# Edge passes of a graph network with one transposed scan per slot, a ring of four row slots and direct indices

## The chip, the cores and the metric

The kernel runs on one core of one Trainium2 chip. The metric is the device time of one execution in microseconds (us). The kernel before takes 10,483.51 us (median of three runs, 10,478.12 to 10,493.6). TensorE, VectorE, ScalarE and GpSimd compute; the Sync, ScalarE and GpSimd queues issue DMAs. Engines are ordered against each other by counting semaphores alone.

## What is computed

Four blocks of a graph network are applied to the same 6,250 nodes of 96 numbers, over 200,000 edges sorted by their destination. Each block's result is added to its input and normalised.

```python
x = _layernorm(x + gat(x, ...))      # attention over edges: softmax by destination, 4 heads of 24
x = _layernorm(x + egnn(x, ...))     # twice: maximum by destination of x[src] @ W_msg + edge_attr @ W_edge
x = _layernorm(x + sage(x, ...))     # twice: mean by destination of x[src]
x = _layernorm(x + gcn(x, ...))      # three times: weighted sum by destination
```

In the attention block an edge's logit is `e = leaky_relu(a_src[src] + a_dst[dst], 0.2)`, and `exp(e - max)` weighs the row `h[src]`, with sum and maximum over the edges of one destination. In the second block `agg = segment_max(x[src] @ W_msg + edge_attr @ W_edge, dst)`.

## The kernel before

The edges are padded to 128 x 1,568: each of the 128 partitions holds 1,568 edges in order of destination. So a running value (maximum, or a weighted sum rescaled when the maximum rises) can go along a partition from edge to edge, and a large negative number in `reset` stops it where a new destination starts. The value behind each edge is stored to DRAM (`hist0`, `hist`), and the row of each node's last edge is gathered from there behind the pass (line 477, 49 indirect DMAs); `carries` then joins what runs over from one partition to the next.

There are three such **gather passes**: the attention pass (q = 0) and two maximum passes (q = 1, 2). A pass works in 196 **slots** of S = 8 edges a partition. For each slot GpSimd issues eight indirect DMAs (line 455), each fetching one row of the node table for each partition, into one of two halves of `G`. Their indices are a copy that ScalarE makes (`idx`, line 923) when it has done the slot's other work, and GpSimd waits for it (line 450) and for VectorE's `rows_used` (line 452).

In an attention slot VectorE adds up the logits (L1341, L1342), runs four scans of eight (L1344), prepares two exponents which ScalarE evaluates (L917), multiplies the eight rows (L1356), and then goes through the eight edges one by one: scale the previous state (L1362), add it (L1365), each step waiting for the one before. The result lies in a second pair of buffers, `H`, which the Sync queue stores (L547). In the first 25 slots VectorE also does a piece of other preparation (`table_piece`).

In a maximum slot there is more. TensorE multiplies eight tiles of edge attributes (L687), which VectorE adds to the gathered rows (L1395), and eight dependent steps `max(previous + reset, row)` follow (L1399). Beside this each slot does four steps (CS = 4) of **counting**: for the later passes the kernel builds a table of how many edges go from a node to a node, as sums of products of one-hot tiles. VectorE compares to make these tiles (L1388, wide, and L1389, narrow), ScalarE makes four scaled identities (L904), TensorE adds three products into PSUM (L666, L667, L672), the third of which takes the previous step's sum, so that ScalarE must have copied this sum (L911) first. Each sum is then flushed to a row of DRAM whose number the Sync queue loads from a table (L541, L542). All engines work in order. The Sync queue's order in a slot is four flushes, the store, the load of the edge attributes for the slot after next (L556).

ScalarE's and GpSimd's passes are loops of the chip; VectorE's and the Sync queue's are written out in full. The seven passes of the mean and graph-convolution blocks behind 8,642 us use the count table and gather nothing.

## Time and profile before

| | us |
|---|---|
| median of three runs | 10,483.51 |
| the profiled execution | 10,478.01 |
| its span | 10,475.3 |
| TensorE, VectorE, GpSimd, ScalarE busy | 4,947.4, 5,313.2, 4,906.2, 1,468.9 |
| DMA moved | 1,134 MB |

The profile divides the span by engine and line, says for each instruction how long its engine had been idle and which event ended this, and gives the order of events in any stretch. "Remote" is what it calls an event whose origin it does not know. A DMA's issue is the queue's work, and its landing a separate event. GpSimd's DMA instructions last about 0.95 us and start 1.25 us apart; the time from start to start is what counts. Three stretches matter: the attention pass from 207 to 2,572 us, and the maximum passes from 2,858 to 5,690 and from 5,812 to 8,642. Behind them TensorE is busy most of the time.

### The profile page before, as it was taken

What the parts mean: (1) busy time and instruction counts of PE and PEld (TensorE: products, weight loads), DVE (VectorE), ACT (ScalarE), POOL (GpSimd) and SP (SyncE); (2) the same over time, 40 slices, a digit from 0 to 9 for tenths busy, and PEclk for the clock granted to TensorE, in tenths of its full rate; (3) what the DMA queues carried; (4) which work ended last, traced back from release to release, by engine and by line L of the source; (5) the groups of instructions that cost most, each with busy time, mean ns of one, the idle gap of its engine ahead of it and who ended that gap; (6) DMA issues with size and microseconds to landing.
All of it is one profiled execution on the core that took longest, in us unless ns stands there. A gap on an engine that the chain in (4) does not pass through costs nothing.

```text
span 10475.3 us, 121795 instructions
## 1 busy us (share of the span) xinstructions
PE 4947.4 (47%) x25358; PEld 3490.2 (33%) x25358; DVE 5313.2 (51%) x17848; ACT 1468.9 (14%) x4065; POOL 4906.2 (47%) x5030
## 2 busy tenths in 40 slices
PE   1100000000355555555554555555555554999999
PEld 1000000000233332322322322322233234999999
DVE  4766665565644444444443544444444446632224
ACT  0000000000122222222221222222222220000000
POOL 6766666666155555555555455555555552000000
PEclk5555555555555555555555555555555557999999
DMA  4322222222033333333332333333333333676666
GB/s 130 87 71 71 72 71 70 72 71 66 27 94 92 92 91 92 92 93 91 92 93 72 89 92 91 94 91 94 92 92 92 92 100 106 217 266 226 227 227 242
DMA packets 605562, 1134.21 MB, mean 108 GB/s; under 512 B 165250, under 2 KB 372501, under 8 KB 604904
## 3 DMA queue, kind: packets, MB, share of 16 engines
q1 hardware_dynamic: 408198, 679.86, 19.3%
q0 software_dynamic: 159184, 251.10, 12.1%
q10 hardware_dynamic: 37906, 200.73, 4.8%
q14 instruction: 240, 1.97, 0.1%
q8 instruction: 34, 0.56, 0.0%
HBM read 716.84 MB, written 414.33 MB: 108 GB/s over the span
## 4 chain that ended last, share of the span: by engine, by line
PE 34%; another core or an unknown queue 27%; DVE 19%; issue 11%; ACT 3%; ACTq 3%; POOL 2%; DMA 1%; DVEq 0%; POOLq 0%; SPq 0%
PE psO L687 7%; PE psB L710 5%; PE psA L710 5%; DVE CG L1365 5%; DVE SCR L1362 5%; PE psX L710 5%; PE psB L672 3%; PE psA L672 2%; PE psA L666 2%; DVE CG L1356 2%; PE psA L667 2%; POOL CG L455 2%; ACT BUF L904 2%; DVE Rm L1344 1%
## 5 line engine op out<-in xcount | busy, mean ns | idle before, releaser
L455 POOL DMA_INDIRECT CG<-table,idx x4704 | 4567.6, 971 | 3678.5 <-issue 1737.8
L1395 DVE TENSOR_TENSOR CG<-CG,psO 128x384 f32<-128x384 f32 x784 | 433.9, 554 | 2475.0 <-remote 2401.0
L672 PE MATMUL psB<-BUF 128*128 128x392 bf16 x784 | 366.2, 467 | 2369.8 <-ACT BUF L911 2279.6
L687 PE MATMUL psO<-WE,BUF 32*128 32x96 f32 x6272 | 1328.8, 394 | 102.4 <-issue 91.9
L687 PEld LDWEIGHTS psO<-WE,BUF 32*128 32x128 f32 x6272 | 1242.9, 298 | 230.6 <-issue 230.6
L1388 DVE TENSOR_SCALAR BUF<-iota,EG 128x392 bf16<-128x392 f16 x3136 | 1050.0, 335 | 221.7 <-issue 160.0
L1399 DVE SCALAR_TENSOR_TENSOR CG<-CG,BUF 128x96 f32<-128x96 f32 x3136 | 1000.8, 319 | 159.0 <-DVE CG L1395 20.2
L672 PEld LDWEIGHTS psB<-BUF 128*128 128x128 bf16 x784 | 81.4, 104 | 2879.3 <-issue 2879.3
L753 PE MATMUL psA<-ident,F 128*100 128x128 f32 x1 | 0.5, 452 | 2091.7 <-DVEq L1320 2091.7
L911 ACT CAST BUF<-psA 128x392 bf16<-128x392 f32 x784 | 381.1, 486 | 3669.8 <-remote 2748.8
L1389 DVE TENSOR_SCALAR BUF<-iota,EG 128x128 bf16<-128x128 f16 x3136 | 771.1, 246 | 6.9 <-issue 6.7
L753 PEld LDWEIGHTS psA<-ident,F 128*100 128x100 f32 x1 | 0.2, 158 | 2092.1 <-DVEq L1320 2092.1
L440 POOL CAST CG<-EG x35 | 26.1, 744 | 1381.1 <-DVEq L1091 1381.1
L1365 DVE TENSOR_TENSOR CG<-CG,SCR 128x100 f32<-128x100 f32 x1568 | 415.4, 265 | 209.9 <-DVE SCR L1362 133.6
L1362 DVE TENSOR_TENSOR SCR<-CG,EX 128x100 f32<-128x100 f32 x1568 | 414.4, 264 | 208.3 <-DVE CG L1365 114.8
L904 ACT ACTIVATE BUF<-ident,EG 128x128 bf16<-128x128 f32 x1568 | 501.5, 391 | 68.0 <-issue 50.9
L710 PE MATMUL psB<-CG,BUF 128*128 128x288 bf16 x4018 | 508.5, 287 | 0.8 <-POOL CG L443 0.8
L710 PE MATMUL psA<-CG,BUF 128*128 128x288 bf16 x4018 | 508.3, 287 | 1.0 <-POOL CG L443 1.0
L710 PE MATMUL psX<-CG,BUF 128*128 128x288 bf16 x3969 | 500.8, 286 | 0.0
L710 PEld LDWEIGHTS psB<-CG,BUF 128*128 128x128 bf16 x4018 | 494.9, 142 | 2.9 <-POOL CG L443 1.1
L710 PEld LDWEIGHTS psA<-CG,BUF 128*128 128x128 bf16 x4018 | 494.8, 142 | 3.0 <-POOL CG L443 1.2
L710 PEld LDWEIGHTS psX<-CG,BUF 128*128 128x128 bf16 x3969 | 488.3, 142 | 1.0 <-POOL CG L443 0.3
(259 smaller groups left out, 5869.2 us busy)
## 6 DMA issues: line engine op xcount, KB each, us to landing
BUF<-counts SPq DMA_DIRECT2D x245, 784.0 KB, 5.8
BUF<-counts ACTq DMA_DIRECT2D x245, 784.0 KB, 6.4
counts<-BUF SPq DMA_DIRECT2D x1572, 98.0 KB
hist<-CG SPq DMA_DIRECT2D x394, 384.0 KB
hist<-CG SPq DMA_DIRECT2D x198, 416.0 KB
CG<-table,idx POOLq DMA_INDIRECT x4704
BUF<-in_edge_attr SPq DMA_DIRECT2D x392, 128.0 KB
table<-TB SPq DMA_DIRECT2D x14, 336.0 KB
```

The source lines that it names most:

```text
L455: pool.indirect_dma_start(out=G[:, s, k * width:(k + 1) * width], out_offset=None, in_=tab, in_offset=bass.IndirectOffsetOnAxis(ap=idx[:, ...
L672: pe.matmul(sums, KI[:, j, :], ACC[:, (j - 1) % CS, :], start=False, stop=True).then_inc(counted, 1)
L687: mm = pe.matmul(ETERM[:, s, k // 4, (k % 4) * DIM:(k % 4 + 1) * DIM], EA[:, s, k, :], WE[:, n0 // ITERS, :], start=True, stop=True)
L710: mm = pe.matmul(sums[:, 0:3 * DIM], CNT16[:, B % 3, b:b + NB * (P - 1) + 1:NB], PARTS[:, b, :], start=b == 0, stop=b == NB - 1, skip_grou ...
L904: nc.scalar.activation(KI[:, j, :], ident[:, :], ACT.Copy, scale=STEP[:, 4, bass.ds(i * (2 * CS) + (s * CS + j), 1)]).then_inc(keep_ready, 1)
L911: nc.scalar.copy(ACC[:, j, :], psM[j % 2][:, 0:CW]).then_inc(acc_ready, 1)
L1362: link(tt(scaled_state[:, :].rearrange("p (h w) -> p h w", w=HW), prev_state(H0, s, k, SW).rearrange("p (h w) -> p h w", w=HW), EX[:, 0, k ...
L1365: link(tt(H0[:, s, k, 0:SW], H0[:, s, k, 0:SW], scaled_state[:, :], ALU.add))
L1388: ts(RHS[:, j, a, :], iota16[:, :], STEP[:, a, column], None, ALU.is_equal).then_inc(onehot_ready, 1)
L1389: ts(LO[:, j, a, :], iota16[:, 0:P], STEP[:, 2 + a, column], None, ALU.is_equal).then_inc(onehot_ready, 1)
L1395: link(tt(HWD[:, s, ks, :], GW[:, s, ks, :], ETERM[:, s, h, 0:4 * DIM].rearrange("p (k w) -> p k w", w=DIM), ALU.add))
L1399: link(stt(HWD[:, s, k, :], prev_state(HWD, s, k, DIM), reset[:, u * S + k:u * S + k + 1], HWD[:, s, k, :], ALU.add, ALU.max))
```

## The change

- The eight dependent steps of a slot become **one scan** over all columns. The slot is laid out transposed, nine elements a column: the last value of the previous slot and the eight new ones. The boundary of a column is a factor of zero (attention) or a large negative reset (maximum), so that one scan instruction runs over 100 x 9 or 96 x 9 elements. VectorE writes its product or addition transposed into `state_cols` or `max_cols`; ScalarE copies the scanned values back into row order (`rows_back`), and spreads resets and factors over the columns (`column_resets`, `head_resets`, `scales`). The four scans of the heads become one, too, and the logits of a slot are computed one slot ahead.
- `G` and `H` become **one ring of four slots**, `ROWS0` or `ROWSW`: the rows are gathered into a slot, the results are written over them, and the slot is stored from there. GpSimd waits only for the landing of the store of four slots ago.
- The gathers take their **indices directly** from the array of sources; `idx` and ScalarE's copy of it go. GpSimd's and ScalarE's passes are written out in full.
- The narrow one-hot tiles of a slot are made by one comparison in place of eight.
- The last two of a slot's four **flushes** are issued by ScalarE behind its sums, in place of the Sync queue, and the row number's range is no longer asserted.

The core of the diff (the old bodies are in the listing above):

```diff
+HOTS = 1 + 2 * CS
+RING = 4
+LAPS = SLOTS // RING
+assert LAPS * RING == SLOTS
+K9 = S + 1
...
+    ROWS0 = CG[:, 0:RING * S * W0].rearrange("p (r k w) -> p r k w", r=RING, k=S)
+    ROWSW = CG[:, 0:RING * S * DIM].rearrange("p (r k w) -> p r k w", r=RING, k=S)
...
+    terms = sb("terms", [P, 2, HEADS, K9])
+    maxima = sb("maxima", [P, 1 + HEADS * K9])
+    max9 = maxima[:, 1:].rearrange("p (h k) -> p h k", k=K9)
+    EX = sb("EX", [P, 2, 2, HEADS, K9])
+    reset_heads = sb("reset_heads", [P, 2, HEADS, K9])
+    spread1 = sb("spread1", [P, DIM * K9])
...
+    state_cols = [STG[:, 0:SW * K9].rearrange("p (c k) -> p c k", k=K9), XTQ[:, 0:SW * K9].rearrange("p (c k) -> p c k", k=K9)]
+    max_cols = [STG[:, 0:DIM * K9].rearrange("p (c k) -> p c k", k=K9), XTQ[:, 0:DIM * K9].rearrange("p (c k) -> p c k", k=K9)]
+    max_flat = [STG[:, 0:DIM * K9], XTQ[:, 0:DIM * K9]]
+    scales_flat = XTQ[:, SW * K9:2 * SW * K9]
+    reset_flat = [XTQ[:, SW * K9:SW * K9 + DIM * K9], spread1[:, :]]
+    reset_cols = [v.rearrange("p (c k) -> p c k", k=K9) for v in reset_flat]
...
-        def gather_pass(q, tab, width):
-            with pool.Fori(0, ITERS) as i:
...
+        def gather_pass(q, tab, rows_in):
+            for u in range(SLOTS):
+                r, lap = u % RING, q * LAPS + u // RING
+                if u >= RING:
+                    pool.wait_ge(hist_stored[r], 16 * lap)
+                for k in range(S):
+                    pool.indirect_dma_start(
+                        out=rows_in[:, r, k, :], out_offset=None, in_=tab,
+                        in_offset=bass.IndirectOffsetOnAxis(ap=SRC[:, u * S + k:u * S + k + 1], axis=0)).then_inc(
+                            gathered[r], 16)
...
-                for j in range(CS):
+                for j in range(CS // 2):
                     k = u * CS + j
                     sp.wait_ge(acc_ready, m * HALF + k + 3)
-                    row = sp.value_load(ADDR[0:1, k:k + 1], min_val=0, max_val=TRASH + BG - 1)
+                    row = sp.value_load(ADDR[0:1, k:k + 1])
                     sp.dma_start(counts16[bass.ds(row, P, BG), :], ACC[:, j, :]).then_inc(flushed[j], 16)
             def store(u):
-                s = u % 2
-                sp.wait_ge(block_done[s], u // 2 + q * ITERS + 1)
-                sp.dma_start(rec[:, u * S * width:(u + 1) * S * width], H[:, s, 0:S * width]).then_inc(hist_stored[s], 16)
+                r, lap = u % RING, q * LAPS + u // RING
+                sp.wait_ge(block_done[r], lap + 1)
+                sp.dma_start(rec[:, u * S * width:(u + 1) * S * width], ring[:, r, :]).then_inc(hist_stored[r], 16)
...
-                    pe.wait_ge(rows_used[s], i + (q * ITERS + 1))
+                    pe.wait_ge(eterm_used, i * 2 + (m * SLOTS + s + 1))
...
+        def count_steps(m, u):
+            k0 = m * HALF + u * CS
+            act.wait_ge(counted, k0 + 1)
             for j in range(CS):
                 nc.scalar.activation(KI[:, j, :], ident[:, :], ACT.Copy,
-                                     scale=STEP[:, 4, bass.ds(i * (2 * CS) + (s * CS + j), 1)]).then_inc(keep_ready, 1)
+                                     scale=STEP[:, 4, u * CS + j:u * CS + j + 1]).then_inc(keep_ready, 1)
             for j in range(CS):
-                act.wait_ge(counted, i * (2 * CS) + (m * HALF + s * CS + j + 2))
-                act.sem_inc(turn["act"], 1)
-                act.wait_ge(flushed[j], i * 32 + 16 * (m * 2 * ITERS + s + 1))
-                act.sem_inc(turn["act"], 1)
+                act.wait_ge(flushed[j], 16 * (m * SLOTS + u + 1))
+                act.wait_ge(counted, k0 + j + 2)
                 nc.scalar.copy(ACC[:, j, :], psM[j % 2][:, 0:CW]).then_inc(acc_ready, 1)
-        def edge_pass(q):
...
+            for j in range(CS // 2, CS):
+                act.wait_ge(acc_ready, k0 + j + 3)
+                row = act.value_load(ADDR[0:1, u * CS + j:u * CS + j + 1])
+                act.dma_start(counts16[bass.ds(row, P, BG), :], ACC[:, j, :]).then_inc(flushed[j], 16)
+        def attention_pass():
+            def head_resets(u):
+                nc.scalar.copy(reset_heads[:, u % 2, :, 1:K9],
+                               reset[:, u * S:(u + 1) * S].unsqueeze(1).broadcast_to([P, HEADS, S])).then_inc(resets_ready, 1)
+            def rows_back(u):
+                nc.scalar.copy(ROWS0[:, u % RING, :, 0:SW],
+                               state_cols[u % 2][:, :, 1:K9].rearrange("p c k -> p k c")).then_inc(block_done[u % RING], 1)
+            act.wait_ge(out_ready, NG)
+            act.wait_ge(pass_begun, 1)
+            head_resets(0)
+            head_resets(1)
+            for u in range(SLOTS):
+                act.wait_ge(exp_in, u + 1)
+                nc.scalar.activation(EX[:, u % 2, :, :, :], EX[:, u % 2, :, :, :], ACT.Exp).then_inc(exp_done, 1)
+                if u + 2 < SLOTS:
+                    head_resets(u + 2)
+                if u:
+                    act.wait_ge(scanned, u)
+                act.wait_ge(exp_done, u + 1)
+                nc.scalar.copy(scales[:, :, 1:K9].rearrange("p (h w) k -> p h w k", w=HW),
+                               EX[:, u % 2, 0, :, 1:K9].unsqueeze(2).broadcast_to([P, HEADS, HW, S])).then_inc(scales_ready, 1)
+                if u:
+                    rows_back(u - 1)
...
+            act.wait_ge(scanned, SLOTS)
+            rows_back(SLOTS - 1)
...
+        def running_pass(f, q):
+            m = MAX_PASSES.index(q)
+            def column_resets(u):
+                nc.scalar.copy(reset_cols[u % 2][:, :, 1:K9],
+                               reset[:, u * S:(u + 1) * S].unsqueeze(1).broadcast_to([P, DIM, S])).then_inc(resets_ready, 1)
+            def rows_back(u):
+                nc.scalar.copy(ROWSW[:, u % RING, :, :],
+                               max_cols[u % 2][:, :, 1:K9].rearrange("p c k -> p k c")).then_inc(block_done[u % RING], 1)
+            act.wait_ge(out_ready, out_group_base(f, "rows") + NG)
+            act.wait_ge(pass_begun, q + 1)
+            act.wait_ge(steps_loaded, 32 * (m + 1))
+            column_resets(0)
+            column_resets(1)
+            for u in range(SLOTS):
+                if u:
+                    act.wait_ge(scanned, q * SLOTS + u)
+                    rows_back(u - 1)
+                    if u + 1 < SLOTS:
+                        column_resets(u + 1)
+                count_steps(m, u)
+            act.wait_ge(scanned, (q + 1) * SLOTS)
+            rows_back(SLOTS - 1)
...
+            def logits(u):
+                r, b = u % RING, u % 2
                 here = slice(u * S, (u + 1) * S)
...
+                z = terms[:, 1, :, 1:K9]
+                dve.wait_ge(gathered[r], 16 * S * (u // RING + 1))
+                link(tt(z.rearrange("p h k -> p k h"), ROWS0[:, r, :, SW:W0], AD[:, here, :], ALU.add))
+                step(stt(z, z, 0.2, z, ALU.mult, ALU.max))
+                dve.wait_ge(resets_ready, u + 1)
+                dve.wait_ge(dve_step, steps[0])
+                link(nc.vector.tensor_tensor_scan(
+                    out=maxima[:, 1:], data0=reset_heads[:, b, :, :].rearrange("p h k -> p (h k)"),
+                    data1=terms[:, 1, :, :].rearrange("p h k -> p (h k)"), initial=0.0, op0=ALU.add, op1=ALU.max))
+                link(tt(terms[:, 0, :, :].rearrange("p h k -> p (h k)"), maxima[:, 0:HEADS * K9],
+                        reset_heads[:, b, :, :].rearrange("p h k -> p (h k)"), ALU.add))
+                tt(EX[:, b, :, :, :].rearrange("p a h k -> p a (h k)"), terms[:, :, :, :].rearrange("p a h k -> p a (h k)"),
+                   maxima[:, 1:].unsqueeze(1).broadcast_to([P, 2, HEADS * K9]), ALU.subtract).then_inc(exp_in, 1)
+                step(nc.vector.tensor_copy(ROWS0[:, r, :, SW:W0], max9[:, :, 1:K9].rearrange("p h k -> p k h")))
+                dve.wait_ge(exp_in, u + 1)
+                step(nc.vector.tensor_copy(terms[:, 1, :, 0:1], max9[:, :, S:K9]))
+            def states(u):
+                r, b = u % RING, u % 2
+                if u >= 2:
+                    dve.wait_ge(block_done[(u - 2) % RING], (u - 2) // RING + 1)
+                dve.wait_ge(exp_done, u + 1)
+                step(tt(state_cols[b][:, :, 1:K9].rearrange("p (h w) k -> p h w k", w=HW),
+                        ROWS0[:, r, :, 0:SW].rearrange("p k (h w) -> p h w k", w=HW),
+                        EX[:, b, 1, :, 1:K9].unsqueeze(2).broadcast_to([P, HEADS, HW, S]), ALU.mult))
+                if u:
+                    dve.wait_ge(scanned, u)
+                step(nc.vector.tensor_copy(state_cols[b][:, :, 0:1], state_cols[1 - b][:, :, S:K9]))
+                dve.wait_ge(scales_ready, u + 1)
+                dve.wait_ge(dve_step, steps[0])
+                nc.vector.tensor_tensor_scan(out=state_flat[b], data0=scales_flat, data1=state_flat[b], initial=0.0,
+                                             op0=ALU.mult, op1=ALU.add).then_inc(scanned, 1)
+            link(nc.vector.memset(scales[:, :, 0:1], 0.0))
+            link(nc.vector.memset(state_cols[1][:, :, S:K9], 0.0))
+            dve.sem_inc(pass_begun, 1)
+            logits(0)
             for u in range(SLOTS):
-                slot(u)
+                if u + 1 < SLOTS:
+                    logits(u + 1)
+                states(u)
...
+                r, b = u % RING, u % 2
                 dve.wait_ge(counted, m * HALF + u * CS + 1)
+                tt(LO, iota16[:, 0:P].unsqueeze(1).unsqueeze(1).broadcast_to([P, CS, 2, P]),
+                   STEP[:, 2:4, u * CS:(u + 1) * CS].rearrange("p a j -> p j a").unsqueeze(3).broadcast_to([P, CS, 2, P]),
+                   ALU.is_equal).then_inc(onehot_ready, 1)
                 for j in range(CS):
-                    column = slice(u * CS + j, u * CS + j + 1)
                     for a in range(2):
-                        ts(RHS[:, j, a, :], iota16[:, :], STEP[:, a, column], None, ALU.is_equal).then_inc(onehot_ready, 1)
-                        ts(LO[:, j, a, :], iota16[:, 0:P], STEP[:, 2 + a, column], None, ALU.is_equal).then_inc(onehot_ready, 1)
-                dve.wait_ge(gathered[s], 16 * S * (q * ITERS + i + 1))
-                dve.wait_ge(hist_stored[s], 16 * (q * ITERS + i + 2))
+                        ts(RHS[:, j, a, :], iota16[:, :], STEP[:, a, u * CS + j:u * CS + j + 1], None,
+                           ALU.is_equal).then_inc(onehot_ready, 1)
+                if u:
+                    dve.wait_ge(scanned, q * SLOTS + u)
+                step(nc.vector.tensor_copy(max_cols[b][:, :, 0:1], max_cols[1 - b][:, :, S:K9]))
+                dve.wait_ge(gathered[r], 16 * S * (q * LAPS + u // RING + 1))
                 dve.wait_ge(eterm_ready[s], m * ITERS + i + 1)
-                for h in range(2):
-                    ks = slice(4 * h, 4 * h + 4)
-                    link(tt(HWD[:, s, ks, :], GW[:, s, ks, :],
-                            ETERM[:, s, h, 0:4 * DIM].rearrange("p (k w) -> p k w", w=DIM), ALU.add))
-                dve.sem_inc(rows_used[s], 1)
-                for k in range(S):
-                    link(stt(HWD[:, s, k, :], prev_state(HWD, s, k, DIM), reset[:, u * S + k:u * S + k + 1],
-                             HWD[:, s, k, :], ALU.add, ALU.max))
-                dve.sem_inc(block_done[s], 1)
+                if u >= 2:
+                    dve.wait_ge(block_done[(u - 2) % RING], q * LAPS + (u - 2) // RING + 1)
+                tt(max_cols[b][:, :, 1:K9].rearrange("p c (a k) -> p c a k", a=2),
+                   ROWSW[:, r, :, :].rearrange("p (a k) c -> p c a k", a=2),
+                   ETERM[:, s, :, 0:4 * DIM].rearrange("p a (k c) -> p c a k", c=DIM), ALU.add).then_inc(eterm_used, 1)
+                dve.wait_ge(resets_ready, q * SLOTS + u + 1)
+                dve.wait_ge(dve_step, steps[0])
+                dve.wait_ge(eterm_used, m * SLOTS + u + 3)
+                nc.vector.tensor_tensor_scan(out=max_flat[b], data0=reset_flat[b], data1=max_flat[b], initial=0.0,
+                                             op0=ALU.add, op1=ALU.max).then_inc(scanned, 1)
+            dve.wait_ge(scanned, (q + 1) * SLOTS)
+            dve.wait_ge(block_done[RING - 1], (q + 1) * LAPS)
```

## Rows read from the trace of the kernel before

**Rows 1.** Table of stages: stretch, its length, busy us of each engine (and count).

```profile
207.00:2572.00 2365.00, 47.31 (x204) 22.53 (x204) 1485.02 (x5603) 78.40 (x392) 1524.83 (x1568) 0.51 0.28 72
...
2858.00:5690.00 2832.00, 1557.38 (x5553) 858.25 (x5553) 1390.64 (x5105) 640.87 (x1764) 1533.35 (x1576) 0.53 0.33 92
```

**Rows 2.** Timeline of GpSimd in a maximum pass: start, length, instruction, [idle before <- releaser].

```profile
4000.46 1.09 POOL L455 DMA_INDIRECT CG<-table,idx  x1 [8.53 <-ACT idx L923]
4001.85 1.17 POOL L455 DMA_INDIRECT CG<-table,idx  x1 [0.30 <-issue]
...
4019.70 0.95 POOL L455 DMA_INDIRECT CG<-table,idx  x1 [0.30 <-issue]
4028.94 1.09 POOL L455 DMA_INDIRECT CG<-table,idx  x1 [8.29 <-ACT idx L923]
```

**Rows 3.** Table of stretches within that cycle, columns as in Rows 1.

```profile
4011.00:4023.30 12.30, 0.36 (x2) 0.00 (x0) 0.00 (x0) 0.00 (x0) 7.51 (x8) 0.50 0.35 95
```

**Rows 4.** Timeline of VectorE (DVE) and ScalarE (ACT) in that cycle.

```profile
4023.34 1.14 DVE L1395 TENSOR_TENSOR CG<-CG,psO 128x384 f32<-128x384 f32 x2 [12.46 <-remote]
4023.52 0.49 ACT L911 CAST BUF<-psA 128x392 bf16<-128x392 f32 x1 [14.01 <-remote]
...
4027.46 0.49 ACT L911 CAST BUF<-psB 128x392 bf16<-128x392 f32 x1 [0.83 <-PE psB L672]
...
4035.89 0.49 ACT L911 CAST BUF<-psB 128x392 bf16<-128x392 f32 x1 [0.67 <-issue]
```

**Rows 5.** Sync queue's flush steps, 4023 to 4030, then 4006 to 4023: ns min/median/max.

```profile
L541 SPq TENSOR_LOAD <-EG x4: 266/286/349, 4024.0 to 4028.0; - x4
L542 SPq DMA_DIRECT2D counts<-BUF x4: 332/338/355, 4024.7 to 4028.8; - x4
...
L542 SPq DMA_DIRECT2D counts<-BUF x3: 699/699/702, 4008.3 to 4021.0; - x3
```

**Rows 6.** Timeline behind the first maximum pass, while GpSimd gathers end rows.

```profile
5690.37 1.86 PE L770 MATMUL psO<-SCR,SEL 128*128 128x96 bf16 x21 [3.94 <-issue]
5718.64 0.86 DVE L1458 TENSOR_TENSOR CG<-psO,cpen 128x672 f32 x1 [28.62 <-remote]
```

**Rows 7.** Timeline of GpSimd in the attention pass.

```profile
1503.86 0.95 POOL L455 DMA_INDIRECT CG<-table,idx  x1 [5.94 <-DVEq L1359]
...
1540.15 0.95 POOL L455 DMA_INDIRECT CG<-table,idx  x1 [6.47 <-DVEq L1359]
```

**Rows 8.** Timeline of VectorE in the same burst, late in it.

```profile
1525.63 0.26 DVE L1362 TENSOR_TENSOR SCR<-CG,EX 128x100 f32<-128x100 f32 x1 [1.13 <-DVE CG L1365]
...
1536.13 0.19 DVE L1347 TENSOR_TENSOR EX<-Rm,BUF 128x32 f32<-128x32 f32 x1 [2.14 <-remote]
```

**Rows 9.** Table of stretches in that burst, columns as in Rows 1.

```profile
1521.40:1537.60 16.20, 0.00 (x0) 0.00 (x0) 4.71 (x21) 0.00 (x0) 9.51 (x10) 0.50 0.25 62
```

**Rows 10.** Costliest groups of the page: count, busy us, mean ns of one, idle before.

```profile
L1395 DVE TENSOR_TENSOR CG<-CG,psO 128x384 f32<-128x384 f32 x784 | 433.9, 554 | 2475.0 <-remote 2401.0
...
L1388 DVE TENSOR_SCALAR BUF<-iota,EG 128x392 bf16<-128x392 f16 x3136 | 1050.0, 335 | 221.7 <-issue 160.0
L1399 DVE SCALAR_TENSOR_TENSOR CG<-CG,BUF 128x96 f32<-128x96 f32 x3136 | 1000.8, 319 | 159.0 <-DVE CG L1395 20.2
...
L1389 DVE TENSOR_SCALAR BUF<-iota,EG 128x128 bf16<-128x128 f16 x3136 | 771.1, 246 | 6.9 <-issue 6.7
...
L1362 DVE TENSOR_TENSOR SCR<-CG,EX 128x100 f32<-128x100 f32 x1568 | 414.4, 264 | 208.3 <-DVE CG L1365 114.8
L904 ACT ACTIVATE BUF<-ident,EG 128x128 bf16<-128x128 f32 x1568 | 501.5, 391 | 68.0 <-issue 50.9
```

**Rows 11.** Groups by shape: VectorE in the first 600 us, then ScalarE.

```profile
L1356 DVE TENSOR_TENSOR CG<-CG,EX 128x800 f32<-128x800 f32 x32 | 31.8, 994 | 2.3 <-DVE Rm L1354 1.2
L1166 DVE TENSOR_TENSOR_SCAN ARENA<-BUF,ARENA 128x1456 f32<-128x1456 f32 x4 | 13.0, 3253 | 0.6
...
L876 ACT COPY STG<-CG 128x672 f32<-128x672 f32 x14 | 10.3, 746 | 112.2 <-DVEq L1474 110.0 <-PE psX L633 2.1
```

160 lines of the change are left out of this document (48 added, 112 removed).

## The prediction

> **What bounds the kernel now.** I read the page, then a table of stages, then one cycle of one stage. The profiled execution took 10,478.0 us with a span of 10,475.3; the median of the timed runs is 10,483.5, 0.05% above. The sum goes against 10,478. By the stage table [rows 1] the attention pass takes 2,365 us and a maximum pass 2,832, and there are two of these: 8,030 of 10,475 us. Each pass has 196 slots, so a slot costs 12.07 us in the one and about 14.3 in the others. No engine is full: in the maximum pass GpSimd is busy 1,533 us, TensorE 1,557, VectorE 1,391, ScalarE 641 [rows 1]. The gathers of a slot start 1.25 us apart (sixteen from 4000.46 to 4020.65, the first two slower at 1.4 [rows 2]); 10.0 us a slot is the floor.
>
> Why is it missed? In the maximum pass GpSimd issues 16 gathers in 20.2 us, pauses 8.3 until ScalarE's index copy, and starts again at 4028.94: a cycle of 28.5 us for two slots [rows 2]. The obvious reading is that the copy is late. But see what the others do inside the burst. From 4011.0 to 4023.3 VectorE and ScalarE do nothing and TensorE 0.36 us, while GpSimd goes on [rows 3]. VectorE's next addition had waited 12.46 us and ScalarE's next sum 14.01, both for something that the profile calls remote, and they start within 0.2 us of each other, 2.7 us after the last gather's end [rows 4]. Meanwhile the Sync queue takes 699 ns for a descriptor step that takes it 338 outside [rows 5]. So news travels slowly; no work is missing. The same is seen behind a pass, where GpSimd issues 49 gathers in a row: VectorE's L1458 waits 28.6 us for a block of 21 matmuls of 1.86 us [rows 6]. I call this the **starving**: while gathers come at 1.25 us without a pause, the other engines' instructions and signals pass at about one in 0.7 us after some time, and about 2.65 us after the last gather it is over. In the attention pass the bursts have 24 gathers, and the next one starts 36.3 us after this one [rows 7]; 17.5 us into it VectorE's linked steps, 0.30 us apart before, have waits of 1.1 and 2.1 us between them [rows 8], 21 instructions in 16.2 us [rows 9].
>
> **A rule for a cycle.** Let W be what the others need for a slot when not starved, L the time from the start of a burst to the standstill, n the slots of a burst. They work during L and again from 2.65 us behind the burst, together nW. So the period is 10.1n + 2.65 + nW - L. Here L = 10.5 and W = (28.5 - 12.3)/2 = 8.1; n = 2 returns 28.5.
>
> **The change, part by part.**
> *Direct indices, four row slots.* ScalarE's index copy, the wait for it and the loops go. A slot may be refilled once its store has landed. GpSimd first runs four slots ahead; then the ring is full, and each refill is released by one stored slot, one each W. The gathers get no cheaper. With W under 10 us the second release comes before the first slot's gathers end, the third (2W = 17) behind the standstill: bursts stay two slots long. The depth moves the phase, not the rate.
> *VectorE, maximum pass.* Before: eight wide and eight narrow comparisons (0.335 and 0.246, but overlapped, 0.39 a pair by starts) 3.15 us, two additions of 0.554, eight steps of 0.319, 0.35 apart: 7.1 us [rows 10]. After: one comparison of 1,024 elements, 1.2 us (384 take 0.554, 100 take 0.264, so about 1 ns each); eight wide ones at 0.23, 1.9; a column copy 0.2; one addition of 768, 0.95; one scan over 96 x 9 = 864 elements, 1.9 (1,456 take 3,253 ns [rows 11], 2.23 each). Sum 6.2, with waits 6.7. Transposed reads may add up to 1 us. VectorE bounds W in neither case, so this is worth nothing.
> *ScalarE, maximum pass.* It gains two transposed copies of 768 elements, 0.84 us each (672 take 0.746 [rows 11]), and two flushes. A flush on the Sync queue runs from a load at 4024.0 to the end of its descriptor step at 4025.04 [rows 5]: 1.04 us, without the range check 1.0. Bounds: 0.34, the descriptor step alone, and 4.2, six steps of 0.7 when starved; I take 1.0, as most of them fall outside the standstill. ScalarE's order is now: last sum, two flushes 2.0, two copies 1.7, four scaled identities, 1.2 at 0.29 a start (0.391 each, overlapped [rows 10]), then four sums 1.25 apart. From last sum to last sum: 0.1 + 2.0 + 1.7 + 1.2 + 3 x 1.25 = 8.7. Before, TensorE's chain ended last, 8.43 from 4027.46 to 4035.89 [rows 4] in a slow-clock slot and 8.1 in the mean. I take W = 8.6, bounds 8.1 and 9.8. Two flushes and two range checks fewer on the Sync queue lie beside this.
> *L.* By my count of the code some 30 of a maximum slot's 190 instructions go, none of TensorE's, which are over 40% of them. I take L = 11.1, bounds 10.5 and 12.
> The period becomes 2 x 18.7 + 2.65 - 11.1 = 28.95, 14.48 a slot against 14.24: 196 x 0.24 = **+45 us** in each maximum pass.
> *Attention pass.* Sixteen linked steps at 0.296, 4.7 us [rows 8, 10], four scans and some small steps go. The new slot of VectorE: 0.99 for a product of 800 elements, 2.0 for one scan of 900 [rows 11], nine small steps at 0.2, 0.5 of waits: 5.3 us instead of 8.4. ScalarE has 0.26 + 0.2 and two copies of 800 at 0.87, one of which stands between two scans: no bound either. Nobody needs 10 us. The starving still comes, since the gathers never pause of themselves: some 14 VectorE instructions at 0.77 (16.2/21 [rows 9]) and the round trip to ScalarE make 12 to 13 us a slot. The ring takes up this 2 to 3 us a slot for about 30 us; then GpSimd waits for a release, that pause ends the starving, and the others catch up. Bounds: 10.03 a slot, and 11.7 if they stand still for a whole ring as in rows 6. I take 10.5: 196 x (12.07 - 10.5) = 308, less some 13 for the fuller ends: **-295 us**.
> Two waits for the last stores at a pass's end delay end gathers that wait for them anyway. Sum: 10,478 - 295 + 2 x 45 = 10,273; I say **10,270**.
>
> *A rule weighed.* Under the comparisons of a maximum slot two gathers take 1.09 and 1.17 us, not 0.95 [rows 2]; that is 0.36 us a slot. The Trainium skill ("SBUF — State Buffer", section "SBUF: two separate sides") has VectorE in a two-port mode lock GpSimd out for the whole instruction. At its worst that would be all 1.9 us of the comparisons, a floor of 11.9 us for a maximum slot; no row shows so much.
>
> **The rivals.**
> *Slower.* ScalarE's chain decides. With W = 9.0 and L unchanged a maximum slot takes 10.1 + 9.0 + (2.65 - 10.5)/2 = 15.2, 392 x 0.93 = +365; with attention at 11.3, -150: 10,690. With W = 9.6 it is 10,930. For it: ScalarE works in order, its flush steps stand ahead of the identities that TensorE waits for, and starved steps cost 0.7 each. Against it: rows 10 give 8.7. It decides from W = 8.9. Chance 0.29, between 10,500 and 10,950.
> *Single bursts.* If a release comes over 2.65 us after a slot's gathers, bursts are of one slot and the standstill hardly begins: at least 10.2 + 2.6 = 12.8 a slot, 392 x 1.44 = -565, with attention -295: 9,620. For it: the store now hangs on ScalarE's copy and on a Sync queue that is slow inside a burst. Against it: a release each 8.6 us is inside 10.1. Chance 0.17.
> *The floor is reached.* If the starving came of the loops, the index hand-over or the four flushes, all passes would run at GpSimd's rate, 10.1 and 10.4: 10,478 - 375 - 2 x 755 = 8,590. Against it stands rows 6, where neither flush nor index copy runs. Chance 0.12. The same page and section of the Trainium skill say that TensorE and ScalarE never wait for anybody at SBUF's ports, which speaks for this rival; rows 3 show them standing still, not why.
> *The forecast*, with its own range of 10,080 to 10,480, has the other 0.42, of which 0.05 lies within 0.2%.
>
> **How the numbers follow.** The time is the forecast's. The range for eight in ten, 9,500 to 10,800, leaves out the floor (0.12), some of the single bursts and the far end of the slower rival. A measurement of this kernel tells about 0.2%, 21 us, from no change. Faster by more: 0.12 + 0.17 + 0.37 of the forecast's 0.42 = 0.66; within: the forecast's other 0.05; slower by more: 0.29.
>
> **What would show it.** In a maximum pass GpSimd still pauses every second slot, now for a store; VectorE and ScalarE still have waits of 10 to 13 us named remote and start together. ScalarE's last sum to last sum is 8.5 to 8.8 us outside the standstill, its transposed copies 0.84, the scan 1.9. The attention pass has bursts far longer than 24 gathers and pauses of 3 to 8 us. The prediction is wrong if the gathers of a maximum pass run unbroken, if the waits named remote are gone, or if sum to sum is over 9.

## The result and the profile after

| | before | changed |
|---|---|---|
| median of four runs, us | 10,488.56 | 9,790.56 |
| ratio, 95% interval | | 0.934, 0.931 to 0.937 |
| span of the profiled execution | 10,475.3 | 9,779.8 |
| VectorE, ScalarE, GpSimd busy, us | 5,313, 1,469, 4,906 | 4,823, 2,776, 5,649 |

The kernel became 6.6% faster where I had forecast 2.0%. By the start of VectorE's first and last instruction of each pass (the logits' addition and the comparisons of line 1444), the attention pass fell from 2,345 to 2,256 us (-89) and the maximum passes from 2,803 each to 2,510 and 2,480 (-293, -322); what lies behind the last pass stayed at about 1,852. My sum had -295 for the one and +45 for each of the others. So both terms were wrong, and opposite ways. The granted clock of TensorE in the maximum passes hardly moved, from 0.53 to 0.54 and 0.55.

The groups of the changed kernel's page: line, engine, operation, shapes and count, then busy time and mean ns, then idle time before. The first answers the gathers of before, 971 ns and 4,567.6 us busy.

```profile
L467 POOL DMA_INDIRECT CG<-table,BUF x4704 | 5310.6, 1129 | 2266.5 <-issue 1416.0
...
L1439 DVE TENSOR_TENSOR BUF<-iota,EG 128x1024 bf16<-128x1024 f16 x392 | 479.7, 1224 | 1060.9 <-PE psB L684 522.1
```

A gather lasts 1,129 ns in the mean and not 0.95 us as in [rows 2]: some are stretched. The timeline of an attention slot shows which:

```profile
1099.09 0.94 POOL L467 DMA_INDIRECT CG<-table,BUF  x1 [0.30 <-issue]
1099.30 1.68 DVE L1400 TENSOR_TENSOR STG<-CG,EX 128x800 f32<-128x800 f32 x1
...
1100.34 1.40 POOL L467 DMA_INDIRECT CG<-table,BUF  x1 [0.30 <-issue]
...
1101.24 2.03 DVE L1408 TENSOR_TENSOR_SCAN STG<-XTQ,STG 128x900 f32<-128x900 f32 x1
1102.05 1.98 POOL L467 DMA_INDIRECT CG<-table,BUF  x1 [0.31 <-issue]
...
1104.33 0.94 POOL L467 DMA_INDIRECT CG<-table,BUF  x1 [0.30 <-issue]
```

The product ends at 1100.98, and the gather begun under it ends at 1101.74, 0.76 later; the scan ends at 1103.27, the gather begun under it at 1104.03, again 0.76 later. The other six gathers take 0.94. This repeats in every slot of the attention pass: 8 gathers and 1.48 us of stretching, 11.46 us a slot (12.02 before), and no pause and no standstill are left. Against [rows 7] and [rows 8], where bursts of 24 gathers ended in slow linked steps, GpSimd never waits here.

In the maximum passes the starving is still there, but rarer. One such place, as timeline: the last stretched gather with the comparison above it, the last gather of the run behind it, and who starts next.

```profile
3514.01 1.23 DVE L1439 TENSOR_TENSOR BUF<-iota,EG 128x1024 bf16<-128x1024 f16 x1 [5.49 <-remote]
...
3514.57 1.47 POOL L467 DMA_INDIRECT CG<-table,BUF  x1 [0.30 <-issue]
...
3543.81 0.94 POOL L467 DMA_INDIRECT CG<-table,BUF  x1 [0.30 <-issue]
3545.63 1.45 DVE L1453 TENSOR_TENSOR XTQ<-CG,psO 128x768 f32<-128x768 f32 x1 [28.10 <-issue]
...
3549.84 0.49 ACT L921 CAST BUF<-psA 128x392 bf16<-128x392 f32 x1 [30.65 <-remote]
...
3559.16 1.96 DVE L1459 TENSOR_TENSOR_SCAN STG<-XTQ,STG 128x864 f32<-128x864 f32 x1
...
3559.56 2.31 POOL L467 DMA_INDIRECT CG<-table,BUF  x1 [14.80 <-DMA hist<-CG]
```

and the busy time of PE, PEld, DVE, ACT and POOL between, in the table of stretches (columns as in Rows 1):

```profile
3519.90:3544.80 24.90, 0.01 (x1) 0.00 (x0) 0.00 (x0) 0.00 (x0) 18.88 (x20) 0.50 0.18 44
```

Behind the stretched gather, which ends at 3516.04, come 23 unstretched ones; 3.9 us later everybody else stops and stands for 25 us, until GpSimd itself runs into the full ring. That is the standstill of [rows 3], twice as long, since the ring is four deep. Two instructions of VectorE stretch gathers here: the one comparison for all narrow tiles (L1439), under which the gather of 3514.57 ends 0.80 us behind it, and the scan (L1459), under which that of 3559.56 takes 2.31 us. In 130 slots of each maximum pass the scan stretched a gather 119 and 125 times, 0.96 us a slot in the mean, and the comparison 87 and 82 times, 0.40 us a slot. But the view of waits, 3000 to 5000 us, counts how often (engine, line and what ended the wait: us, times, longest). First of the kernel before, then of the changed one:

```profile
ACT BUF L911 <- remote: 979.5, 69, 15.8
DVE CG L1395 <- remote: 865.6, 70, 14.2
...
POOL CG L455 <- ACT idx L923: 576.2, 71, 8.6
```

```profile
ACT BUF L921 <- remote: 618.8, 93, 30.7
...
POOL CG L467 <- DMA hist<-CG: 233.5, 24, 15.3
```

GpSimd's pauses fell from 71 to 24 in 2,000 us, and ScalarE's waits named remote from 980 to 619 us, though there are more of them. (VectorE's wait of 28.10 us above is named "issue" by the profile.) The question for the experiments was therefore: did the stretched gathers break the starving, or did the smaller number of instructions, the missing loops or the direct indices?

For all runs I worked out the same figures from 1,040 gathers in a row of each maximum pass, from within slot 47 to within slot 177: the time a slot; the **short breaks**, which is what the starts lie apart beyond 1.248 us, summed over all that are under 4 us apart, per slot; and the **long pauses**, those of 4 us and more, in 130 slots. Instructions are those of all engines in the trace, the sequencers' included. The values are means of both passes. What was expected of the runs was written before this table; where it reckons with 13.5 us for a maximum slot of the changed kernel, the table has 12.85. Runs for which no interval is given were executed once; four executions of one kernel lay up to 0.6% apart, and the paced kernel came out 1.1% apart on two occasions, so smaller differences between single runs are not read.

| kernel | instructions a slot | short breaks, us a slot | long pauses | us a slot |
|---|---|---|---|---|
| before | 182 | 0.34 | 65 | 14.37 |
| before_narrow | 182 | 0.40 | 65 | 14.41 |
| before_direct | 179 | 0.35 | 63 | 13.88 |
| short_pieces | 156 | 0.25 | 63 | 14.65 |
| pieces_small_breaks | 159 | 0.54 | 53 | 14.46 |
| before_idle_scan | 184 | 0.96 | 52 | 13.70 |
| pieces_paced | 160 | 1.08 | 40 | 14.00 |
| depth_two | 139 | 1.13 | 39 | 13.82 |
| flushes_on_sync | 138 | 1.38 | 18 | 12.76 |
| changed kernel | 139 | 1.46 | 16 | 12.85 |
| idle_small_instructions | 159 | 1.46 | 20 | 13.05 |
| breaks_once | 140 | 1.71 | 11 | 12.54 |
| paced_after | 142 | 2.25 | 0 or 1 | 12.26 |
| paced_timed, the same kernel | 142 | 2.02 | 0 or 1 | 12.03 |
| before_paced | 188 | 2.72 | 0 | 12.70 |

### The profile page after: what moved, and what is told of

The parts are those of the page before. It is cut to its first block, busy times and chain, and to the rows that moved or that the text cites. A ratio compares the mean times of both kernels' runs of the same rounds, so it can differ in the third digit from the quotient of the medians.

```text
span 9779.8 us, 100402 instructions
## 1 busy us (share of the span) xinstructions
PE 4893.9 (50%) x25358; PEld 3302.2 (34%) x25358; DVE 4822.7 (49%) x8842; ACT 2776.2 (28%) x4849; POOL 5648.8 (58%) x5030
## 4 chain that ended last, share of the span: by engine, by line
PE 28%; POOL 28%; another core or an unknown queue 16%; issue 13%; ACT 7%; DVE 4%; ACTq 2%; DMA 1%; SPq 0%; DVEq 0%; POOLq 0%
POOL CG L467 27%; PE psB L722 5%; PE psA L722 5%; PE psX L722 5%; PE psO L699 3%; ACT CG L972 3%; PE psB L684 2%; PE psA L684 2%; ACT BUF L921 2%; PE psO L654 1%; ACTq L925 1%; PE psB L678 1%; ACT BUF L916 1%; PE psA L678 1%
## 5 line engine op out<-in xcount | busy, mean ns | idle before, releaser
L467 POOL DMA_INDIRECT CG<-table,BUF x4704 | 5310.6, 1129 | 2266.5 <-issue 1416.0
L699 PE MATMUL psO<-WE,BUF 32*128 32x96 f32 x6272 | 1216.2, 369 | 97.1 <-issue 81.8
L699 PEld LDWEIGHTS psO<-WE,BUF 32*128 32x128 f32 x6272 | 1140.0, 276 | 225.7 <-issue 225.7
L1439 DVE TENSOR_TENSOR BUF<-iota,EG 128x1024 bf16<-128x1024 f16 x392 | 479.7, 1224 | 1060.9 <-PE psB L684 522.1
L1444 DVE TENSOR_SCALAR BUF<-iota,EG 128x392 bf16<-128x392 f16 x3136 | 846.9, 340 | 0.0
L684 PE MATMUL psA<-BUF 128*128 128x392 bf16 x784 | 376.8, 481 | 519.7 <-ACT BUF L916 338.6
L921 ACT CAST BUF<-psB 128x392 bf16<-128x392 f32 x784 | 381.0, 486 | 843.9 <-remote 311.7
L1379 DVE TENSOR_TENSOR terms<-CG,ARENA 128x32 f32<-128x32 f32 x196 | 46.4, 237 | 1140.7 <-DMA CG<-table,BUF 1140.7
L1453 DVE TENSOR_TENSOR XTQ<-CG,psO 128x768 f32<-128x768 f32 x196 | 288.8, 1474 | 620.4 <-issue 497.5
L1453 DVE TENSOR_TENSOR STG<-CG,psO 128x768 f32<-128x768 f32 x196 | 290.3, 1481 | 594.6 <-issue 508.7
```

The costliest lines, as they stand in the source:

```text
L467: pool.indirect_dma_start(out=rows_in[:, r, k, :], out_offset=None, in_=tab, in_offset=bass.IndirectOffsetOnAxis(ap=SRC[:, u * S + k:u * S ...
L684: pe.matmul(sums, KI[:, j, :], ACC[:, (j - 1) % CS, :], start=False, stop=True).then_inc(counted, 1)
L699: mm = pe.matmul(ETERM[:, s, k // 4, (k % 4) * DIM:(k % 4 + 1) * DIM], EA[:, s, k, :], WE[:, n0 // ITERS, :], start=True, stop=True)
L921: nc.scalar.copy(ACC[:, j, :], psM[j % 2][:, 0:CW]).then_inc(acc_ready, 1)
L1439: tt(LO, iota16[:, 0:P].unsqueeze(1).unsqueeze(1).broadcast_to([P, CS, 2, P]), STEP[:, 2:4, u * CS:(u + 1) * CS].rearrange("p a j -> p j a ...
L1444: ts(RHS[:, j, a, :], iota16[:, :], STEP[:, a, u * CS + j:u * CS + j + 1], None, ALU.is_equal).then_inc(onehot_ready, 1)
```

## The experiments

### The first four: breaks against the rest of the change

**short_pieces** cuts VectorE's long instructions (the product, the scan of the maximum pass and the narrow comparison in the same way):

```diff
+                for c in range(0, SW, 10):
+                    cut = slice(c * K9, (c + 10) * K9)
+                    part = nc.vector.tensor_tensor_scan(out=state_flat[b][:, cut], data0=scales_flat[:, cut],
+                                                        data1=state_flat[b][:, cut], initial=0.0, op0=ALU.mult, op1=ALU.add)
...
+                for c in range(0, DIM, 12):
+                    part = tt(max_cols[b][:, c:c + 12, 1:K9].rearrange("p c (a k) -> p c a k", a=2),
...
```

> The changed kernel with every long VectorE instruction of a slot cut into pieces of some 90 to 130 elements: the scan into 11 (attention) or 8 (maximum), the product and the addition into 8, the narrow comparison into 4. Same elements, same hand-overs, same direct indices, ring and flushes. Theory A (the starving still exists, and in the changed kernel it is broken by gathers that a long VectorE instruction stretches to 1.4 to 2.3 us): the stretched gathers go, the starving comes back, the attention slot rises from 11.5 to 12 us or more and a maximum slot from 13.5 to over 14.3: 10,150 to 10,500 us. Theory B (the starving came of the loops, the index hand-over and the many small instructions, and the stretched gathers are only a cost): attention 10.4, maximum 12.3 a slot: about 9,050 to 9,300 us.

Measured: 10,639 us, above the kernel before (10,506 beside it) and 139 us above my range for theory A. All else of the change was in it: scan, ring, indices, flushes. Theory B falls. In the attention pass short breaks fell to 0.23 us a slot and 31 long pauses came back in 130 slots, 12.04 us a slot. In a maximum pass, from 3000 to 5000 us, ScalarE's remote waits are longer in sum again than in the changed kernel, and GpSimd waits 10 us in a cycle of 30:

```profile
ACT BUF L921 <- remote: 759.5, 168, 15.2
```

```profile
4010.48 0.95 POOL L467 DMA_INDIRECT CG<-table,BUF  x1 [10.05 <-DMA hist<-CG]
...
4040.54 1.03 POOL L467 DMA_INDIRECT CG<-table,BUF  x1 [10.06 <-DMA hist<-CG]
```

**before_paced** and **paced_after** add a fill on GpSimd, the first in all passes, the second in the maximum passes (there with 380 columns):

```diff
+                        if k % 4 == 3:
+                            nc.gpsimd.memset(gap[:, :], 0.0).then_inc(gap_made, 1)
+                            pool.wait_ge(gap_made, i * 4 + (q * 4 * ITERS + s * 2 + k // 4 + 1))
+                            pool.sem_inc(turn["pool"], 1)
```

> The kernel before; in all three gather passes GpSimd fills 400 columns of a spare tile after every fourth gather and waits for this (0.5 to 1 us, twice a slot). Only work is added, and none to VectorE. Theory A: breaks in the gathers are enough, whoever makes them: no standstills, 10.0 + 1.0 to 2.0 a slot: 9,000 to 9,700 us. Theory B: added to the bursts of GpSimd, 1 to 2 us a slot: 10,480 to 11,300 us. If the idle scan helps and this does not, it is VectorE's instruction and not the break that matters.

Measured: 10,031 us. It is out of my range for theory A, since the attention pass became 203 us slower (a slot 12.99, short breaks 3.01). The maximum passes, though, went from 2,803 to 2,475 and 2,478. That is the kernel before with nothing but work added, none of it on VectorE. Its gathers and fills:

```profile
4018.00 0.95 POOL L457 DMA_INDIRECT CG<-table,idx  x1 [0.30 <-issue]
4018.95 0.45 POOL L462 MEMSET gap<- 128x400 f32 x1
4020.21 1.07 POOL L457 DMA_INDIRECT CG<-table,idx  x1 [0.81 <-issue]
```

A fill with its wait puts the next gather 2.2 us behind the last one instead of 1.25. In its view of waits, again 3000 to 5000 us, none of the nine largest is named remote; VectorE now waits for rows, as it should:

```profile
DVE CG L1401 <- DMA CG<-table,idx: 725.5, 152, 7.0
```

> The changed kernel; in the maximum passes GpSimd fills 380 columns of a spare tile after every fourth gather and waits for this (some 0.5 to 1 us, twice a slot). Only work is added. Theory A: these breaks do what the stretched gathers do, at a fixed distance, so the remaining standstills and pauses of 9 to 15 us go and a slot costs 10.0 + 1.4 (stretched) + 1.0 to 2.0 instead of 13.5: 9,250 to 9,700 us. Theory B: the breaks add their 1 to 2 us a slot where GpSimd is the bound and are hidden in its pauses elsewhere: 9,800 to 10,500 us.

Measured: 9,581 us, in the range of theory A. No long pause but one is left, a maximum slot takes 12.26 us.

**before_idle_scan** puts one line at the end of each slot of the kernel before:

```diff
+            link(nc.vector.tensor_tensor_scan(out=STG[:, 0:900], data0=BUF[:, T:T + 900], data1=BUF[:, T:T + 900],
+                                              initial=0.0, op0=ALU.mult, op1=ALU.add))
```

> The kernel before with one idle scan over 900 elements (2.0 us of VectorE) at the end of each of the 588 slots; its result is not used. Only work is added. Theory A: it stretches one or two gathers a slot and so breaks the bursts; the standstills of 12 us in a maximum pass go and a slot costs 11 to 12.5 us instead of 14.3, the attention slot 11 to 12.5 instead of 12.1: 9,300 to 10,000 us. Theory B: VectorE's slot grows by 2 us, on the path in attention and partly in the maximum passes: 10,700 to 11,600 us.

Measured: 10,219 us, between the two ranges and 287 below the kernel before. Two us of useless work in each of 588 slots made it faster; A has the sign, but I overrated one break a slot. Long pauses fell only from 65 to 52. The standstills that are left are 5 to 11 us long.

### How many breaks, and what makes the queue slow

**breaks_once** is paced_after with the condition `k == 3`, **flushes_on_sync** moves the loop over the last two flushes from ScalarE back, **depth_two** changes one wait, **before_narrow** one operand:

```diff
-                    pool.wait_ge(hist_stored[r], 16 * lap)
+                    pool.wait_ge(hist_stored[(u - 2) % RING], 16 * (q * LAPS + (u - 2) // RING + 1))
...
-                            out=G[:, s, k * width:(k + 1) * width], out_offset=None, in_=tab,
+                            out=G[:, s, k * width:k * width + (24 if q else width)], out_offset=None, in_=tab.rearrange("n (a w) -> (n a) w", a=4) if q else tab,
```

> The changed kernel with one fill of 380 columns by GpSimd behind the fourth gather of each maximum slot, in place of the two of the run with fills after every fourth gather (9,581 us, 12.45 us a slot in its steady part, of it 0.8 for the fills). If one break a slot, together with the stretched gather, is enough: 0.4 us a slot less, 12.05, so 9,400 to 9,450 us. If breaks must come every four gathers: standstills come back, 9,600 to 9,800 us.

Measured: 9,702 us, in the second range. One fill a slot is not enough; 11 long pauses stay.

> The changed kernel with all four flushes of a maximum slot on the Sync queue again; ScalarE issues none. ScalarE's slot becomes about 1 us shorter (8.9 to some 8.0 from sum to sum), the Sync queue's 1.3 to 2 us longer. Theory A: GpSimd's gathers with their stretching and what is left of the starving set the pace, not ScalarE's chain: 9,700 to 9,850 us, within 1% of the changed kernel. Rival: ScalarE's chain sets it, as my sum had it: 9,400 to 9,600 us. Second rival: the Sync queue crawls first inside a burst, and its two flushes more delay the stores: 9,900 to 10,300 us.

Measured: 9,789 us against 9,791 of the changed kernel, in the range of theory A. ScalarE's two flushes are worth nothing either way, and the rival by which its chain sets the time falls.

> The changed kernel; GpSimd waits for the landing of the store of two slots ago instead of four, so that the ring is used two deep. If depth only moves the phase, as my prediction had it, and with more pauses even less starving comes: 9,600 to 9,850 us. If the way from a gather to its stored slot (addition, scan, copy back one slot later, store, landing; 12 us and more) has to be covered: the attention slot goes from 11.5 to 13 or more, a maximum slot from 13.5 to 14 or more: 10,100 to 10,800 us.

Measured: 12,142 us, far above both ranges. In the attention pass the slots run in lockstep, 21.7 us each, and the gathers wait 12 us for each store:

```profile
1507.71 0.95 POOL L467 DMA_INDIRECT CG<-table,BUF  x1 [12.02 <-DMA hist<-CG]
...
1516.46 0.95 POOL L467 DMA_INDIRECT CG<-table,BUF  x1 [0.30 <-issue]
1529.41 0.95 POOL L467 DMA_INDIRECT CG<-table,BUF  x1 [12.01 <-DMA hist<-CG]
```

VectorE computes the logits of slot u + 1 ahead of the states of slot u, and so cannot finish u before the rows of u + 1 have come. A ring of two leaves no slot to gather into meanwhile. A maximum slot rose by 1.0 us. The depth is thus a condition of the change, and my sentence that it only moves the phase was wrong. I had reckoned a refill to be released each W; a ring this short puts the whole way of a slot, from gather to stored rows, between two refills.

> The kernel before; in the maximum passes a gather fetches 24 numbers a row in place of 96 (its result is therefore not the reference's). The count of gathers, of descriptors and of signals is the same, the bytes a quarter. If the starving comes of the bytes that the gathers move: the standstills of 12 us go, and with them some 400 us in each maximum pass: 9,500 to 9,900 us. If it comes of issuing the gathers (descriptors and signals): the standstills stay 11 to 13 us, and the time stays within 10,300 to 10,500 us.

Measured: 10,515 us, 20 above the kernel before beside it and 15 above the second range. From 3000 to 5000 us the gathers' queue moved 13.7 MB in place of 54.9 with as many packets, and the standstill is the same:

```profile
4017.90 1.14 DVE L1395 TENSOR_TENSOR CG<-CG,psO 128x384 f32<-128x384 f32 x2 [12.17 <-remote]
4018.10 0.49 ACT L911 CAST BUF<-psA 128x392 bf16<-128x392 f32 x1 [13.85 <-remote]
```

So the starving does not hang on the bytes that are fetched. What in the issuing causes it, none of these runs shows.

### Trying to have the breaks cheaper

> The changed kernel with VectorE's long instructions cut into pieces (alone this gave 10,639 us) and with GpSimd's fill of 380 columns after every fourth gather, now in all three passes. Theory A: the pieces take the stretching away (1.4 to 1.6 us a slot), the fills take over as breaks (0.8 us a slot), so an attention slot costs 11.1 us (11.5 in the changed kernel) and a maximum slot 11.1 to 11.4 (12.45 in the paced kernel): 9,000 to 9,150 us. If the stretched gathers themselves are needed, standstills stay: 9,500 to 10,500 us.

Measured: 10,216 us (10,200 to 10,265), ratio 0.974 with 0.971 to 0.977. Theory A failed by over 1,000 us; the time lies in the other range. I had taken two fills a slot for sufficient because paced_after had no pauses. But there they stood beside 1.4 us of stretching. Alone, with some 0.26 left of that, they come to 1.08 us a slot, and 40 long pauses stay. That the stretched gathers themselves are needed, the other reading, doesn't hold: before_paced has no long scan and no long pause. It was this run that led me to the table above: the long pauses go with the sum of the short breaks, across kernels with 139 to 188 instructions a slot. The table orders the kernels; that the sum alone decides, and not also where in the run of gathers the breaks lie, is not shown.

> The same with fills of 8 columns in place of 380, so that the break between gathers is the fill's signal and little more (some 0.1 to 0.2 us longer than no break, against 0.4). If any break is enough: 0.4 us a slot less than with 380 columns, 8,850 to 9,000 us. If a break has to leave the queue some time: the starving comes back in part, 9,200 to 10,600 us.

Measured: 10,597 us (10,584 to 10,647), ratio 1.011, 1.008 to 1.014. Smaller breaks, 0.54 us a slot, more pauses. That fits the second expectation.

### One part alone, and the number of instructions

**before_direct**: the kernel before with its gather passes written out and `SRC[:, u * S + k:u * S + k + 1]` as index; ScalarE's copy and both waits stay.

> The kernel before with one part of the change alone: GpSimd's gather passes written out in full, with their indices straight from the array of sources. ScalarE's copy and GpSimd's two waits stay. Theory A: loops and the indices' place have nothing to do with the starving; the bursts of 16 and the standstills of 12 us stay, 10,440 to 10,520 us. Theory B (loops or copied indices cause it): the standstills go, 9,500 us or less.

Measured: 10,265 us, 232 less than the kernel before beside it, and neither theory had it. The bursts of 16 are all there. But the first gather comes sooner behind ScalarE's copy:

```profile
4015.08 0.20 ACT L922 COPY idx<-BUF 128x8 int32 x1
...
4015.55 0.98 POOL L454 DMA_INDIRECT CG<-table,BUF  x1 [7.73 <-ACT idx L922]
```

0.47 us, where in [rows 2] the gather of 4028.94 starts 1.10 us behind the copy of 4027.84. GpSimd's long pauses are 7.3 us in the mean instead of 8.1, and two of 65 are gone: a maximum slot takes 0.49 us less, 192 us over 392 slots. So part of the gain has nothing to do with scans. The run changed three things at once, GpSimd's loop, its waits against registers and the place of the indices; which of them it is, isn't shown. How much of this is left in the changed kernel, which has no copy to wait for, wasn't separated.

> The changed kernel with 20 idle VectorE instructions (one column each, some 0.1 us) at the end of each of the 588 slots; they are too short to hold up a gather by much. A maximum slot then has some 160 instructions instead of 139, an attention slot 47 instead of 27. If the breaks alone decide: the attention slot stays at 11.5 us and the 130 slots in the middle of a maximum pass keep 14 to 20 long pauses: 9,780 to 9,900 us. If the count of instructions is a cause of its own: the attention pass has pauses over 4 us again, and a maximum pass over 25: 10,000 to 10,400 us.

Measured: 9,899 us, a slot with 159 instructions instead of 139, short breaks equal. The attention slot stays at 11.5 with no pause; the long pauses in the maximum passes rise from 16 to 20, the slot by 0.20 us. That is my first case, at its upper end. Taken at its word it is 0.01 us an instruction, so the 43 fewer of the change would be worth at most 0.4 us of the 1.5 that a maximum slot gained. But the paced kernel alone differs by 0.23 us a slot between its two runs. So the number of instructions is a small cause or none; which of the two stays open.

> The kernel with two fills a maximum slot once more, now timed in three rounds. From its one look, 9,581 us: a ratio of 0.913 to the kernel before, with an interval of 0.003 to either side; the changed kernel has 0.934.

Measured: 9,476.66 us, ratio 0.904 with 0.9025 to 0.9055. It beats both kernels, the changed one by 3%. Its first run had been 1% higher, and so the ratio lies below the one that I expected. There the short breaks were 2.25 us a slot and here 2.02: the scans lay differently to the gathers. Why, isn't shown.

## Why the prediction was wrong

**What bounds the kernel**: right. The starving was there as described, the remote waits are gone where it is gone, and adding work removed it. "No work is missing" is what before_paced shows: a maximum slot of 12.7 us with all the work of before.

**VectorE's part**: the scan was right (1.96 us against 1.9; in attention 2.03 against 2.0), and so was the narrow comparison (1.22 against 1.2). The product and the addition were not: 1.68 instead of 0.99, and 1.48 instead of 0.95. They read the rows across, neighbours 104 or 96 elements apart, and write them in columns of nine; this new order is the likely cause, and my margin of 1 us for it holds. I called this part "worth nothing", as VectorE bounds no slot. **Here lies the error that decides.** The change turns 16 or 8 linked steps of 0.3 us into one scan of 2 us, lengthens the product from 0.99 to 1.68 us and makes one comparison of 1.22 us out of eight of 0.25, and these hold GpSimd up; the maximum pass's addition does not. I saw it in [rows 2] under the comparisons, gathers of 1.09 and 1.17 us, and wrote it down as a cost of 0.36 us, "at its worst" 1.9. I never asked what a delayed gather does to the starving, though my own rule says that the starving ends once gathers pause. A delayed gather is both: a cost of 1.4 us a slot and, in the maximum passes, the cure of a greater loss. With the long instructions cut (short_pieces) a maximum slot takes 14.65 us, with them 12.85: a net gain of 1.8 us, where my sum had nothing.

**L**: I reckoned with a standstill that begins 11.1 us into each burst, a little later since some 30 of 190 instructions go. By the trace 43 of 182 went, and idle_small_instructions shows this to be worth little; what moved the standstill were the breaks. The 14.24 us a slot from which I counted came from one cycle of 28.5 us; the mean is 14.37.

**ScalarE's part**: the sum held and its terms did not. Outside a standstill the last sums follow each other at 8.88 us against 8.7 in my sum:

```profile
3562.62 0.49 ACT L921 CAST BUF<-psB 128x392 bf16<-128x392 f32 x1 [0.72 <-PE psB L684]
3563.07 1.14 ACTq L925 DMA_DIRECT2D counts<-BUF  x2
3564.26 1.59 ACT L972 COPY CG<-STG 128x768 f32<-128x768 f32 x1 [1.15 <-issue]
3565.75 0.83 ACT L968 COPY XTQ<-BUF 128x768 f32<-128x768 f32 x1
...
3571.50 0.49 ACT L921 CAST BUF<-psB 128x392 bf16<-128x392 f32 x1 [0.72 <-PE psB L684]
```

The two flushes take 1.14 us (I had 2.0), the copy back takes 1.59 (I had 0.84, from copies that transpose nothing), the spread of the resets 0.83. But W had no weight: a slot takes 12.85, not 8.9. flushes_on_sync shows the same.

**The rule for a cycle** failed where it took bursts to be two slots long. It has no term for short breaks; with them, a burst is as long as the breaks let it be, 28 gathers without a break at times, and 65 between two long pauses in the mean (16 pauses in 1,040 gathers).

**Attention**: "the gathers never pause of themselves" was wrong for the same reason. 11.46 lies within my bounds of 10.03 and 11.7, on the way of the one mechanism that I had not counted. I took 10.5, a sum without any delay of a gather.

**The rule weighed**: that VectorE can hold GpSimd up matters more in these traces than I let it. The Trainium skill ("SBUF — State Buffer", section "Who interferes with whom") says besides that a VectorE instruction with two inputs in SBUF contends with a GpSimd instruction that reads there, while it infers that `tensor_tensor` leaves the making of a DMA's descriptors alone. The trace agrees with the first: product, scan and narrow comparison, all with both inputs in SBUF, stretch a gather, which takes its indices from SBUF. It differs from the second, for the gather under the product (a `tensor_tensor`) took 1.40 us and not 0.94, and the measurement decides. The maximum pass's addition, whose second input is PSUM, does not:

```profile
3504.94 0.94 POOL L467 DMA_INDIRECT CG<-table,BUF  x1 [0.30 <-issue]
3504.96 1.47 DVE L1453 TENSOR_TENSOR STG<-CG,psO 128x768 f32<-128x768 f32 x1 [4.26 <-DMA CG<-table,BUF]
3506.19 0.94 POOL L467 DMA_INDIRECT CG<-table,BUF  x1 [0.31 <-issue]
```

I had read only the rule on the two-port mode. For two inputs in SBUF a term was due in my sum; product and scan together measured 1.48 us a slot in the attention pass. That the delay would help in the maximum passes, no page says.

**The rivals.** Slower (0.29): W came out at 8.9, the point from which it was to decide, and it decided nothing. Single bursts (0.17): 9,620 was near to the result, from another mechanism; GpSimd does not pause every slot. The floor (0.12): in attention the gathers ran without a pause, as it had them, but at 11.46 us a slot with the stretching and not at 10.1. The range held the time; the forecast's own range did not.

**The sum again**, by measured terms: attention (11.46 - 12.02) x 171 slots = -96 (the first 25 carry other work), against -89 by the stage's length. Maximum (12.85 - 14.37) x 392 = -596, against -616. The three stages' lengths come to -705 us; the stretches between the passes grew by 11, which leaves the -695 us of the span.

## What to carry to other kernels

An engine that issues without a pause can slow all others, and then its own next release is late; count what a stall of it costs, and also what it gives the others. Before adding an instruction of over 1 us on VectorE beside GpSimd's gathers, look at whether both its inputs lie in SBUF: here all three such instructions stretched a gather, and the one with an input in PSUM did not. When everybody stands still and nobody is full, adding a small pause to the one that runs is a cheap and telling experiment.

## What the runs showed of the hardware that I had not expected

- While gathers start 1.25 us apart without a break, TensorE, VectorE and ScalarE come to a stop after some time (3.9 us in the place shown above, 10.5 in the cycle of [rows 2] and [rows 3]) and stand until the gathers pause: 25 us in that place. Short breaks of 2.0 us a slot with 142 instructions, and of 2.7 with 188, prevented it. For the attention pass with 27 or 47 instructions, 1.5 us were enough; 1.0 us with 46 left 12 long pauses in 130 slots. A quarter of the bytes changes nothing (14.41 us a slot against 14.37). What carries the news so slowly remains open.
- A gather held up by a VectorE instruction ends 0.75 us behind the scan, 0.76 behind the product and 0.82 behind the narrow comparison, whatever it had waited.
- Reading rows across and writing them in columns of nine goes with longer instructions on VectorE: an addition over 768 elements 1.48 us, a product over 800 1.68 us, against 0.99 for a product of 800 in the order of the rows [rows 11]. ScalarE's copy of 768 elements from nine apart takes 1.58 us, its spread of eight numbers over 768 places 0.83.
- GpSimd's gathers started 0.6 us sooner after their release (0.47 us behind ScalarE's copy in place of 1.10) without a loop, without register waits and with indices from another tile; the three weren't separated.
